# A gated cross-attention and mixture-of-experts layer: the shared expert's weights are prepared and loaded at another place, the last additions stand half a tile elsewhere

## The reference, cut to what matters

```
x = x + tanh(g_xattn[0]) * xattn(layernorm(x), ctx, ctx)
xt = layernorm(x)
probs, ids = softmax over the top 2 of (xt @ Wr + br + gate_bias)
expert(e): u = xt @ Wup[e] + bup[e]
           g = silu(u @ Wgate[e] + bgate[e]) * u
           g @ Wdown[e] + bdown[e]
x = x + tanh(g_ffn[0]) * (sum over the two ids of probs * expert(id) + shared expert)
```

## Time and profile before

| What | Value |
|---|---|
| median of 3 runs | 1298.67 us (1296.82 to 1299.84) |
| the profiled execution's own time | 1291.94 us |
| its span, first to last instruction | 1290.0 us |
| busy: PE, DVE, ACT, POOL | 1199.0, 853.2, 586.1, 376.1 us |
| chain that ended last, by engine | PE 72%, DVE 12%, issue 5%, DMA 4%, POOL 4%, ACT 2% |
| mean granted TensorE clock | 0.975 |

### The profile page before, as it was taken

One profiled execution on the slowest core, in us unless ns is written; L12 is line 12 of the kernel. 1 busy time (PEld: TensorE's weight loads), 2 busy tenths in 40 slices (PEclk: granted clock), 3 DMA queues, 4 the chain that ended last, 5 costly groups with the idle time before them and its releaser, 6 DMA issues.

```text
span 1290.0 us, 40478 instructions
## 1 busy us (share of the span) xinstructions
PE 1199.0 (93%) x15170; PEld 894.9 (69%) x15170; DVE 853.2 (66%) x1471; ACT 586.1 (45%) x1131; POOL 376.1 (29%) x453
## 2 busy tenths in 40 slices
PE   3888889999777999999999999999999999999996
PEld 2444445555367777778888888888888888877774
DVE  5889989999776789545545445444444444448887
ACT  3767779898776422233333333333333333322221
POOL 4457666666710000210111111111111011015553
PEclk9889999999977999999999999999999999999998
DMA  5765556565566231644322453226411142267765
GB/s 189 222 226 179 177 177 213 192 208 191 178 215 227 66 131 66 221 159 144 115 81 81 155 182 136 65 65 213 144 58 57 54 151 88 68 198 233 243 189 162
DMA packets 91602, 197.36 MB, mean 153 GB/s; under 512 B 12177, under 2 KB 12689, under 8 KB 91537
## 3 DMA queue, kind: packets, MB, share of 16 engines
q1 hardware_dynamic: 80816, 161.34, 36.6%
q0 software_dynamic: 10720, 35.14, 9.4%
HBM read 332.72 MB, written 64.49 MB: 308 GB/s over the span
## 4 chain that ended last, share of the span: by engine, by line
PE 72%; DVE 12%; issue 5%; DMA 4%; POOL 4%; ACT 2%; DVEq 1%; SPq 0%; ACTq 0%; POOLq 0%
PE PS L1629 41%; PE PS L1667 20%; DVE negm L981 6%; PE PS L1614 3%; PE PS L1449 2%; PE PS L1483 1%; DMA xnd<-xhl 1%; DMA qB<-negT 1%; PE PS L1469 1%; POOL whl L674 1%; DVE wst L1010 1%; DVE xn L967 1%; PE PS L1565 1%; DMA yg<-ysl,ixf 1%; DVE rec L994 1%
## 5 line engine op out<-in xcount | busy, mean ns | idle before, releaser
L1629 PE MATMUL PS<-xT,wb 128*128 128x128 f16 (+1 forms) x4128 | 279.8, 229 | 4.5 <-issue 2.4
L1629 PE MATMUL PS<-uhl,wb 128*128 128x128 f16 (+1 forms) x4128 | 279.8, 229 | 1.9 <-DVE uhl L1239 1.9
L1629 PEld LDWEIGHTS PS<-xT,wb 128*128 128x128 f16 x4128 | 264.0, 98 | 14.0 <-issue 5.4
L1629 PEld LDWEIGHTS PS<-uhl,wb 128*128 128x128 f16 x4128 | 263.5, 98 | 10.8 <-DVE uhl L1239 1.4
L1667 PE MATMUL PS<-wb,ghl 128*128 128x512 f16 x1200 | 267.2, 379 | 0.0
L1667 PEld LDWEIGHTS PS<-wb,ghl 128*128 128x128 f16 x1200 | 115.9, 98 | 130.1
L900 ACT ACTIVATE sl<-PS,bb 128x128 f32<-128x128 f32 (+1 forms) x344 | 106.9, 388 | 188.2 <-PE PS L1629 186.1
L890 ACT ACTIVATE u<-PS,bb 128x128 f32<-128x128 f32 (+1 forms) x344 | 107.0, 388 | 171.5 <-PE PS L1629 166.9
L724 POOL COPY ixr<-idx 128x2 int32 (+1 forms) x35 | 6.4, 184 | 610.5 <-PE PS L1614 610.5
L981 DVE TENSOR_REDUCE negm<-PS 128x8 f16<-128x1024 f32 x128 | 155.1, 1212 | 22.4 <-PE PS L1449 21.5
L1246 DVE TENSOR_TENSOR g<-sl,u 128x512 f32<-128x512 f32 x102 | 70.5, 691 | 150.3 <-ACT sl L900 150.3
(11 more groups left out here) (157 smaller groups left out, 1391.2 us busy)
## 6 DMA issues: line engine op xcount, KB each, us to landing
wb<-wsc SPq DMA_DIRECT2D x219, 1024.0 KB
wst<-in_wall SPq DMA_DIRECT2D x32, 768.0 KB, 5.9
wsc<-whl SPq DMA_DIRECT2D x32, 768.0 KB, 4.3
ysl<-yb SPq DMA_DIRECT2D x43, 512.0 KB
bd<-in_bdown SPq DMA_DIRECT2D x74, 256.0 KB
X<-in_x SPq DMA_DIRECT2D x8, 1024.0 KB, 6.6
qB<-qT SPq DMA_DIRECT2D x32, 256.0 KB, 2.6
xnd<-xhl SPq DMA_DIRECT2D x32, 256.0 KB, 3.3
```

The lines of the kernel that those rows point to most:

```text
L1629: ins = pe.matmul(bank_of(bank, t, m, kind), wb[:, j, l, k, w, m * P:(m + 1) * P], rhs(x, k)[:, ts], start=(n == 0), stop=(n == len(TERMS) ...
```

## The change

Four things change, in one text.

- The block that `load_w` reads and `store_w` writes at step b is block b - 4, and at steps 0 to 3 it is 28 to 31: the shared expert comes first.
- The three loads of the shared expert's layers into `wb` go from between the stores of `xhl` to SP's body of the last batch, ahead of the store of block 30 of the sequence, behind waits that `C`, `xn32` and `qx` are no longer read.
- The low half of the last block on DVE goes from ahead of the first `four` to behind it; its store on SP from behind the first four stores of `xhl` to behind the first twelve. The biases are loaded behind 24 stores of `xhl`. ACT waits for attention's end and the last block's store ahead of the first expert tile.
- In the late tiles `add_routed` of the first two batches moves ahead by half a tile: into tile 43's middle instead of its end, and so on; the last tile keeps the last two batches alone.

```diff
             def load_w(b, par):
-                sp.dma_start(wst[:, par, :, :], a["wall"][b]).then_inc(w_in[par], 16)
+                sp.dma_start(wst[:, par, :, :], a["wall"][block_of(b)]).then_inc(w_in[par], 16)
...
+            def shared_weights():
+
+                for j in range(2):
+                    sp.wait_ge(w_out[j], 16 * KT // 2)
+                sp.wait_ge(S["tq_done"], NB)
+                sp.wait_ge(S["va_ready"], NB)
+                sp.wait_ge(S["kh_ready"], NB)
+                sp.wait_ge(S["k_split"], NB)
+                sp.wait_ge(S["q_split"], NB)
+                for l in range(3):
+                    load_layer(l, E_R, 0, {})
...
+                if isinstance(half, int) and number(half, par) == NB - 1:
+                    shared_weights()
...
-            store_x2(0)
+            for i in range(3):
+                store_x2(i)
             store_w(NB // 2 - 1, 1, True)
-            store_x2(1)
-
             sp.wait_ge(S["x1_ready"], NB)
-            for par in range(2):
-                sp.wait_ge(w_out[par], 16 * (NB // 2))
-            first_layer(0, 0)
+            for i in range(3, 6):
+                store_x2(i)
             for par in range(2):
                 load_bias(E_R, par, 0, always)
-            for l in range(1, 3):
-                store_x2(2 * l)
-                store_x2(2 * l + 1)
-                first_layer(l, 0)
...
-            v.wait_ge(S["whi_ready"], NB)
-            v.wait_ge(S["wlo_ready"], NB - 1)
-            v.tensor_tensor(whl[:, 1, :, 1, :], wst[:, 1, :, :], whl[:, 1, :, 0, :], ALU.subtract).then_inc(S["wlo_ready"], 1)
-
             def four(i, last):
...
             four(0, False)
+
+            v.wait_ge(S["whi_ready"], NB)
+            v.wait_ge(S["wlo_ready"], NB - 1)
+            v.tensor_tensor(whl[:, 1, :, 1, :], wst[:, 1, :, :], whl[:, 1, :, 0, :], ALU.subtract).then_inc(S["wlo_ready"], 1)
...
-                if isinstance(late, int) and late == 1:
-                    add_routed(0, 1)
-                elif late is not None and not isinstance(late, int) or late in (2, N_TILES - 1 - SH_B0):
+                if isinstance(late, int) and late < 2:
                     add_routed(late, 0)
+                if late is not None and following is not None and not (isinstance(late, int) and late == 0):
+                    add_routed(late, 1)
+                if late is not None and following is None:
+                    routed_first(late)
                 if following is not None:
                     split_u(i + 1, 1 - par, following)
...
-                if following is None:
-                    routed_first(late)
                 down_out(i, par, kind, half)
...
-                    if isinstance(late, int) and late < 2:
-                        add_routed(late, 0)
-                    if not (isinstance(late, int) and late == 0):
-                        add_routed(late, 1)
+                    if isinstance(late, int) and late == 0:
+                        add_routed(0, 1)
+                    else:
+                        add_routed(late + 1, 0)
```

More of the change, by code:

```diff
@@ L320, in _, with block_of @@
         def _(sp):
+            def block_of(b):
+                return (b + NB - KT) % NB if isinstance(b, int) else b - KT
             def load_w(b, par):
-                sp.dma_start(wst[:, par, :, :], a["wall"][b]).then_inc(w_in[par], 16)
+                sp.dma_start(wst[:, par, :, :], a["wall"][block_of(b)]).then_inc(w_in[par], 16)
             xv = a["x"].rearrange("b p d -> p b d")
@@ L363, in store_w @@
                 sp.wait_ge(S["wlo_ready"], b + 1)
-                sp.dma_start(wsc[bass.ds(b, 1)].rearrange("o l p r -> (o p) l r"),
+                sp.dma_start(wsc[bass.ds(block_of(b), 1)].rearrange("o l p r -> (o p) l r"),
                              whl[:, par, :, :, :].rearrange("p l h c -> p l (h c)")).then_inc(w_out[par], 16)
@@ L374, in _, with load_layer @@
             sp.dma_start(C[:, n:NB, :], ctxv[:, n:NB, :]).then_inc(c_in[1], 16)
+            def load_layer(l, e, j, cond):
+                sp.dma_start(wb[:, j, l, :, :, :].rearrange("p k h c -> p k (h c)"),
+                             wsc.rearrange("(e k) l p r -> e l p k r", k=KT)[bass.ds(e, 1), l].rearrange("o p k r -> (o p) k r"), **cond).then_inc(wl_in[l][j], 16)
+            def shared_weights():
[8 more added lines that the diff above has]
+                    load_layer(l, E_R, 0, {})
             def body(half, par, quad):
@@ L397, in other @@
                 return {"cond": sp.value_load(chg[0:1, back - 1, t, bass.ds(j, 1)], min_val=0, max_val=1)}
-            def load_layer(l, e, par, cond):
-                sp.dma_start(wb[:, par, l, :, :, :].rearrange("p k h c -> p k (h c)"),
-                             wsc.rearrange("(e k) l p r -> e l p k r", k=KT)[bass.ds(e, 1), l].rearrange("o p k r -> (o p) k r"), **cond).then_inc(wl_in[l][par], 16)
             def load_bias(e, par, s, cond):
@@ L462, in _ @@
                 store_y(i, i % 2)
+                if i == 0:
+                    for par in range(2):
+                        sp.wait_ge(w_out[par], 16 * (NB // 2))
                 if i < 3:
@@ L902, in gate_out @@
                     ins.then_inc(S["s_ready"], 1)
+            act.wait_ge(S["x1_ready"], NB)
+            act.wait_ge(S["wlo_ready"], NB)
             evac_x(0, 0)
+            for par in range(2):
+                act.wait_ge(w_out[par], 16 * (NB // 2))
             up_out(0, 0, "early", 0)
```

## The result

The changed kernel took 1287.97 us (median of 12 runs, 1284.2 to 1293.64), the kernel before 1297.28 us (12 runs, 1292.36 to 1300.68): ratio 0.9932, 95% interval 0.9912 to 0.9952, some 9 us less (6.2 to 11.4). The prediction was 1291.4 us, or -7.3; the range 1286.0 to 1297.0 holds the time. The profiled execution has a span of 1284.4 us against 1290.0.

A forecast was written before the change was run, and what follows sets the result against it. PE, with 72% of the chain, was taken as the bound and untouched; the change acts where PE is not last. Norm -6.9, late tiles +5.1, end -5.5 make -7.3 us: 1298.67 to 1291.4 us, range 1286.0 to 1297.0.

The forecast's parts named there:

- The loads' new place: Second layer norm: loads queued ahead delay the first store of `xhl`; ACT waits 0.4 to 3.8 us, taken as 2.1.
- the low half: Second layer norm: the last block's low half on DVE, behind eight batches, costs 0 to 1.76 us, taken as 0.5.
- my 6.9: Second layer norm: ACT's waits for stores fall from 12.6 to 5.7 us, a gain of 6.9 us.
- The last block's store: Second layer norm: it now stops the stores behind twelve others, costing 1.0 to 2.79 us, taken as 1.9.
- The biases: Second layer norm: four bias loads, no longer hidden beside the first load, cost 0 to 2.5 us, taken as 1.2.
- The late tiles: From tile 43: earlier additions wait for gathers and refills; loss 5.1 us, ends 0.8 and 8.3.
- rival 4: Tile 44's layer two: TensorE's clock falls in the new wait, priced at 2.0 us; 1293.4 us, chance 13%.
- the signs of being wrong: Longer `qB` or `wst` waits, ACT waits over 10 us, `yg` waits in tiles 46 to 49, late-tile clock under 1.00.
- The end: Last tile: four additions leave it and the wait for the last gather goes; gain 5.5 us, ends 3.7 and 6.3.
- Rival 1: Late tiles: refills never catch up and additions wait in every tile, 23.2 us lost; 1309.5 us, chance 9%.
- rival 2: Second layer norm: the loads come back as other waits, leaving 1.8 us of gain; 1296.5 us, chance 14%.
- rival 3: Late tiles: they heal at once, only the first 4.5 us wait stays, loss 0.8; 1287.1 us, chance 14%.

The follow-up runs named there:

- The half that was to gain: Changed kernel with the late tiles' routed additions back in their old places, leaving the weights' part; ratio 0.9936 to the kernel before.
- second-buffer kernel: Changed kernel plus a second buffer of gathered rows in the late tiles, its order of additions kept; ratio 0.9918 to the kernel before.
- both (115.9 us for the late tiles): Changed kernel with two buffers of gathered rows and the late additions spread, at most two pairs per half tile; ratio 0.9857 to the kernel before.
- the spread order alone: Changed kernel with the late pairs of additions spread over the half tiles, single buffer of gathered rows; ratio 0.9925 to the kernel before.
- The old order: Late additions placed as before the change; with a second buffer of gathered rows on the changed kernel, ratio 0.9892 to the kernel before.
- additions-alone kernel: Kernel before with only the late tiles' routed additions moved to their new places; ratio 1.0024 to the kernel before.

## Why the prediction was right, point by point

- **The sign and the sum.** -7.3 was forecast, -8.4 is the sum of the stretches and -9.3 the difference of the medians; the interval holds all three. The half that was to gain gained alone (0.9936). The other half, forecast at -0.4, lost 3.1 us alone (0.8 to 5.3). So there is luck in the sum: the norm's stage gave more than forecast, and that offsets late tiles that cost more, most of all in the profiles with the long waits.
- **The loads' new place.** Forecast: the first stores of `xhl` 2.1 late and 0.5 more for the low half. Measured: 1.27, and 1.02 that the low half can't have made; in three other kernels the low half's wait was 0.6. I charged each load 3.7 us of the queue, from the landing of the row maxima on. SP issued the first load 0.79 us behind their issue, and the windows show 349 and 356 GB/s from 345 to 356 us, 3.9 MB, which is the loads and the block's store: some 3.0 us a load. The landing of 5.7 us behind a load, from which I took 3.7, holds more than the load's share of the queue. The Trainium skill (DMA: Bandwidth & Descriptors, Specifications), whose limit of some 358 GB/s I weighed and left, is near these two windows; but the earlier trace rows has one of 375, and in the second-buffer kernel 351.05 to 356.05 us shows 384, so it is no bound here. The waits fell by 7.7, between my 6.9 and the 8.2 that I estimated by that page; the 0.9 us that make it 8.65 are in neither.
- **The last block's store** was put at 1.9 and cost 0.29 (0.26 to 0.84 in the other profiles with it there): behind stores that landed after 2.0 to 2.2 us ACT had slack. **The biases** were put at 1.2, by the time that SP takes to issue them, and cost 2.37: SP spent 2.0 us on issuing them, and the store behind them landed 4.6 us after its issue, where it takes 2.0 without them. The two errors nearly cancel. Moving the biases showed theirs (norm -2.4); moving the low half and the store back to their old places showed what the new ones save (3.1).
- **The late tiles.** The chain of waits was followed to within 0.2 us for two tiles: layer two of 44 and 45 stand 21.05 and 41.06 us behind that of 43, forecast 21.0 and 40.9. Tile 46 is 59.05 (58.4), 47 is 75.61 (74.9). Two things were under-sized. The clock fell (0.66), as rival 4 has it and as I had listed among the signs of being wrong: layer two of tile 44 took 1.67 us more. Tile 45's wait for rows hid that, here and in the other three profiles of this order (layer two of tile 45 stands 40.3 to 41.1 us behind that of tile 43 in all four). And the refills' waits vary: ahead of the copy of `xT` in tile 45 DVE waits 0.67 us for rows here, and 0.45, 2.04 and 4.16 in the others; behind the two long ones layer one of tile 46 comes 2.68 and 4.45 us late and takes 7.08 for 5.40. Four profiles put the term at 5.5 to 10 instead of 5.1, so the 5.75 here is near the lucky end. I gave the clock 13% as a case by itself, and it is a part of the wait.
- **The end.** -5.5 forecast, -5.37 measured, and DVE ends 2.06 us behind PE (2.1).
- **One attribution was incomplete, without harm.** In the 3.66 us that the old late tiles lost I named a wait for the gather. The larger part, 2.01, is two pairs of additions ahead of the copy of `xT`; the price was read from the row and stayed right.
- Rival 1 (refills never catch up) is excluded by the tiles from 46 on (16.56 and 16.55); rival 2 (loads come back as waits) by the 4.9 us; rival 3 by tile 45.

## What to carry to other kernels

Ask of a moved transfer what it lands next to: the loads' new place, in an empty stretch of the queue, was worth most of 5.6 us, and that with four loads of biases (0.5 MB together) at a place where they cost 2.4. A wait put ahead of dense matmuls can cost its length and then the clock, so price them as one: here those of 2.7 to 4.5 us were followed by 1.67 to 2.79 us of slow matmuls, one of 2.01 in two kernels and not in a third, and those of 1.9 us and less were not. Where a buffer is refilled behind its user, order and depth have to be changed together: against both (115.9 us for the late tiles), the spread order alone left 5.7 us, the second buffer with the changed kernel's order 5.5, and neither 8.5. The old order left some 3 us, with one buffer or with two.

## What was not expected of the hardware

With the same code the granted clock at attention's end differs between profiles, and shifts the norm's stretch by some 2 us (66.74 and 67.05 in two kernels, 64.5 to 65.0 in four others with the same norm's code). In the two, ACT's first normalised rows start 9.07 us behind the first cut, in the four 7.26 to 7.47. The ten us behind that cut, of the changed kernel, then of the spread order with one buffer:

```profile
344.91:354.91 10.00, 6.48 (x48) 1.97 (x41) 4.77 (x9) 8.20 (x12) 6.28 (x6) 1.00 1.02 358
```

```profile
347.76:357.76 10.00, 9.65 (x42) 2.46 (x44) 2.95 (x6) 6.19 (x9) 4.26 (x3) 0.50 0.94 328
```

PE does the same stage's work there at 1.2 GHz (0.50) and the others wait for it. From 20 to 10 us ahead of the cut both have the clock at 1.00, with PE busy for 8.8 of the ten us. The additions-alone kernel was at 0.50 ahead of its cut as well, but had the full clock back from five us behind it on, and its norm stretch is no longer than before (73.29 for 73.45). What makes the clock fall in one execution and not in another was not tried.
